# Output projections of blocks 0 and 1, in quarters between the last value products of attention

## The chip, the core and the metric

The kernel runs on one core of a Trainium2 chip. Its engines are named as the profile names them: PE (TensorE; PEld is its weight load), DVE (VectorE), ACT (ScalarE), POOL (GpSimd) and SP (SyncE, which here issues DMAs). The metric is the device time of one execution in microseconds; lower is better.

## The reference

A transformer block on x of shape (4, 2048, 256), all in float32. What matters here is its middle:

```python
h = layernorm(x) * (1 + ca) + sa
# attention: 16 heads of width 16, causal softmax, q and k with rope
y = einsum('bhqk,bhkd->bhqd', softmax(q k^T / 4), v)
x = x + ga * (y.reshape(b, t, 256) @ Wc)          # the output projection
h = layernorm(x) * (1 + cb) + sb
# router: 12 experts (8 with a feed-forward of 512, 4 "zero" ones), top 2
x = x + gb * ffn(h)
```

## The kernel before, in words

Four phases follow one another, each one block of instruction streams per engine, closed by a barrier of all engines (line 978 is the barrier that closes attention's): `project` (norm, q, k, v), `attention`, `route` (output projection, residual, norm, router, sort by expert) and `experts`.

**Attention** works through 16 iterations (4 batch entries x 4 groups of 4 heads). One iteration has 40 tiles of 128 keys by 512 queries: 4, 8, 12 and 16 tiles for the four query ranges of 512, the last four of each range on the diagonal, 512, 384, 256 and 128 queries wide. For a tile PE writes scores (line 1199, four products in strips of 32 rows for each head, one PSUM bank for 512 columns; three banks in turn, 0 to 2), ACT takes the exponential into SBUF (line 1247; one for each bank), POOL masks a diagonal tile (line 1127), and PE adds the tile's value product into bank 3 (line 1215: four heads, 8 records, as each float32 product shows twice). Scores wait for the exponential three banks back. After a query range ACT copies bank 3 (line 1239) and SP stores it (line 1026). Row maxima for the softmax are found beforehand by products into banks 4 to 7 (line 230) and reductions on DVE (line 243); those of the last iteration end long before its last tiles. The order of scores, value products and maxima on PE is a list, `course.pe_order`, which a planner (`Course`) writes from estimated costs; SP's pieces (loads and stores) are hung on value products by `PIECES`. In the last iteration these are the loads for routing: for each of blocks 0 to 3 of 512 tokens, two loads of attention's outputs (line 1474) and one of the rows of x (line 1493), behind value products 1, 4, 7, 10 and so on up to 35. The list ends:

```
scores(36,3) scores(37,0..3) scores(38, heads 0-1) values(36)
scores(38, heads 2-3) scores(39, all heads) values(37) values(38) values(39)
```

Up to value product 35 the four sets of one tile stand between two value products, as in the rows below: values(32), scores(33,3), scores(34,0), (34,1), (34,2), values(33).

Behind the list PE projects block 0 (`projected`, line 1486): for each of its four quarters of 128 tokens two products of 128 x 128 by 128 x 256 in float32 (4 records), into banks 4 and 5. It first waits for the weights (`wc_done`), the loads of block 0 and the last reduction. SP ends its stream with waits for its stores, those of the reciprocals of the softmax sums (line 1013) among them.

**Routing** takes 16 blocks of 512 tokens. PE's order in step s is: projection of block s (line 1611; even blocks into banks 4 and 5, odd ones into 6 and 7), router logits of block s-3 (line 1628), transposes of the normed block s-2 (line 1619). `output(0)` is empty, as attention has done that work. A projection waits for its loads and, from block 2 on, for DVE's residual of the block two before. DVE adds the residual (line 1687, waits for `out_done`), takes statistics, and shifts the normed block (line 1680) after ACT (line 1779) and POOL (line 1820). SP loads block 4 once `out_done` counts 1 and block 5 once it counts 2, each behind its stores of earlier blocks.

Of the kernel before, what the change touches and what calls it, by code (L numbers as in the profile page):

```python
# [31 lines left out]
B, T, C = 4, 2048, 256  # L32
H, L, DH = 16, 64, 16
KC = C // P
# [5 lines left out]
TPB = BLK // P  # L40
# [4 lines left out]
NIT = B * NG  # L45
# [28 lines left out]
ZTERMS = [GROUPS_OF[2][:2], GROUPS_OF[2][2:], GROUPS_OF[0] + GROUPS_OF[1]]  # L74
part_of = [p for p, n in enumerate(PARTS) for _ in range(n)]
XB, XR = 4, 6
BIG = 1e30


def apart(eng):  # L80

    eng.nop(nofuse=True)
# [794 lines left out]
def attention(nc, a, d, k, ps, g0, first, retired):  # L877
    with ExitStack() as ctx:
# [15 lines left out]
        NKT = len(KT)  # L894
# [49 lines left out]
        num, x_in = routed_inputs(k)  # L944
# [13 lines left out]
        red_ready, red_done = g0["red_ready"], g0["red_done"]  # L958
# [19 lines left out]
        with nc.Block() as block:  # L978
# [185 lines left out]
            @block.tensor  # L1164
            def _(pe):
                def group(n, u, at):

                    r = n % R
                    if u == 0:
                        pe.wait_ge(ld[r], LD * (n // R + 1))  # L1170
                    if at >= NRED:
                        pe.wait_ge(red_done, at - NRED + 1)
                    unit_products(pe, k, ps, ks[r], qs[r], u, at).then_inc(red_ready, 1)

                def turn(n, q, at):

                    pe.wait_ge(part_step, PART * (NJ * n + q + 1))
                    pe.wait_ge(red_done, at - NRED + 1)
                    apart(pe)
                    o = red_ps[0:MROWS * QUARTER, at % NRED, 0, :].bitcast(BF16)  # L1180
                    rows = mparts[:, q, :, :, :].rearrange("p h m i -> p (h m i)")
                    for lo in range(0, MROWS * QUARTER, SLOT):
                        part = slice(lo, min(lo + SLOT, MROWS * QUARTER))
                        ins = pe.transpose(o[part, 0:P], rows[:, part], k["identb"][:, :])
                    ins.then_inc(red_ready, 1)

                def scores(n, r, s):

                    m, h0, nh = SETS[s]
                    J, j, lo = KT[m]  # L1190
                    o = st_view(r, s)
                    if s == 0 and 0 < n < R:
                        pe.wait_ge(ones_ld, 16 * (R - 1))
                    if h0 == 0 and j == 0:
                        pe.wait_ge(m_ld, M_LD * (NJ * n + J + 1) + 1)
                    pe.wait_ge(exp_done, NSET * n + s + 1)
                    for h in range(nh):
                        for at_q in QUADS:
                            ins = pe.matmul(o[at_q, h, :], ks[r][0:SROWS + MROWS, h0 + h, j * P + at_q.start:j * P + at_q.stop],  # L1199
                                            qs[r][0:SROWS + MROWS, h0 + h, J * QJ + lo:(J + 1) * QJ], start=True, stop=True)  # L1200
                    ins.then_inc(st_ready, 1)

                def values(n, r, m):

                    J, j, lo = KT[m]
                    if m == 0:
                        pe.wait_ge(v_ld[r], 16 * NV * (n // R + 1))
                    if j == 0:
                        pe.wait_ge(o_done, NJ * n + J + 2)
                    if m in DIAG:  # L1210
                        pe.wait_ge(mask_done, len(DIAG) * n + DIAG.index(m) + 1)
                    else:
                        pe.wait_ge(exp_done, NSET * n + of_tile[m][-1] + 1 + NST)
                    for g in range(HG):
                        ins = pe.matmul(o_ps[SLOT * g:SLOT * (g + 1), lo:QJ], vs[:, r, j, SLOT * g:SLOT * (g + 1)],  # L1215
                                        probs[:, (NKT * r + m) % NPB, g, 0:QJ - lo], start=(j == 0), stop=(m == LAST[J]))
                    ins.then_inc(pv_done, 1)

                for kind, n, x in course.pe_order:
                    if kind == "scores":  # L1220
                        scores(n, n % R, x)
                    elif kind == "values":
                        values(n, n % R, x)
                    elif kind == "turn":
                        turn(n, x, unit_at[n, TURN + x])
                    elif n > 0 or x >= HEAD:
                        group(n, x, unit_at[n, x])
                pe.wait_ge(wc_done, B)
                pe.wait_ge(first["o"][0], 16 * KC)
                pe.wait_ge(red_done, len(course.stream))  # L1230
                apart(pe)
                projected(pe, k, projected_bank(ps, 0), num, 0).then_inc(first["out"][0], 1)

            @block.scalar
            def _(act):
# [241 lines left out]
def projected_bank(ps, j):  # L1477

    return ps[:, 4 + 2 * j:6 + 2 * j, :].rearrange("p n (j c) -> p (n j) c", j=2)


def projected(pe, k, o, num, t):

    for n in range(TPB):
        for c in range(KC):
            ins = pe.matmul(o[:, n, :], num[:, t % XB, c, n * P:(n + 1) * P], k["wc"][:, t // BPS, c, :],
                            start=(c == 0), stop=(c == KC - 1))
    return ins
# [7 lines left out]
def route(nc, a, d, k, r, w, w_in, w_ld, ps, out, scat, first, retired):  # L1496
    with ExitStack() as ctx:
# [41 lines left out]
        with nc.Block() as block:  # L1539
# [61 lines left out]
            @block.tensor  # L1601
            def _(pe):
                def output(t):
                    if t == 0:
                        return
                    pe.wait_ge(o_ld[t % XB], 16 * KC * (t // XB + 1))
                    if t >= RAW:
                        pe.wait_ge(y_done, t - RAW + 1)
                    if t >= 2:
                        pe.wait_ge(mid_done, t - 1)  # L1610
                    projected(pe, k, pc[t % 2], num, t).then_inc(out_done, 1)

                def normed(t):
                    pe.wait_ge(mod_done, t + 1)
                    if t >= 1:
                        pe.wait_ge(ht_done, t)
                    for n in range(TPB):
                        for c in range(KC):
                            ins = pe.transpose(pd[:, n, c, :], r["h2"][:, TPB * t + n, c * P:(c + 1) * P], k["ident"][:, :])
                    ins.then_inc(tr_done, 1)  # L1620

                def logits(t):
                    pe.wait_ge(ht_done, t + 1)
                    if t >= 1:
                        pe.wait_ge(lgb_done, t)
                    for n in range(TPB):
                        for c in range(KC):
                            ins = pe.matmul(pl[:, n, :], h2_t[:, n, c, :], k["gate"][:, c, :], start=(c == 0), stop=(c == KC - 1))
                    ins.then_inc(lg_done, 1)

                def counts(*parts):
                    def stage(t):
                        for p in parts:
                            if t == LASTS[p]:
                                pe.wait_ge(c_ld, 16 * len(CONSTS))
                                pe.wait_ge(oh_done, p + 1)
                                if p > 0:
                                    pe.wait_ge(pos_done, 2 * p)
                                chains[p].counts(pe, r, bank).then_inc(cnt_mm, 1)
                    return stage  # L1640

                def weights(lo, hi):
                    def stage(t):
                        e = t - (NB - E)
                        if not lo <= e < hi:
                            return
                        for half in range(4):
                            m, h, n = half // 2, half % 2, 4 * e + half
                            if h == 0:
                                pe.wait_ge(w_ld[m][e % 2], 16 * (e // 2 + 1))  # L1650
                            if n == 0:
                                pe.wait_ge(mid_done, NB)
                            if n >= 4:
                                pe.wait_ge(wt_copy, n - 3)
                            for q in range(4):

                                at = (q * KC + h) * P if m == 0 else ((q % 2) * FC + 2 * h + q // 2) * P
                                ins = pe.transpose(ps[:, 4 + half, q * P:(q + 1) * P], w_in[:, e % 2, m, at:at + P], k["ident"][:, :])
                            ins.then_inc(wt_done, 1)
                    return stage  # L1660

                blocks((6, counts(0, 2)), (AT + 1, counts(1)), (0, output), (3, logits), (8, weights(0, 1)), (2, normed), (8, weights(1, E)))
# [521 lines left out]
```

## Time and profile before

| | us |
|---|---|
| median of 3 runs | 2433.78 |
| lowest, highest | 2430.32, 2438.25 |
| the profiled execution, whole | 2438.3 |
| its span | 2436.6 |
| PE busy, share of the span | 2294.7, 94% |
| DVE, ACT, POOL busy | 1875.3, 1675.1, 727.1 |
| mean granted clock of PE | 0.975 of 2.4 GHz |

All rows below come from the one profiled execution, counted in microseconds from the start of its span. A product's record runs over the start of the next one, since products are pipelined: the time that PE gives to a group is read from its start to the start of what follows. In a timeline, the bracket at the end gives the idle time of the engine ahead of the row and what ended it; "PEq L978" is the closing of attention's barrier. In windows the columns are width, then for each engine busy time and (x) number of records, then granted clock, share of the DMA engines and GB/s; if one engine is named, its busy time stands alone. Attention ends at some 1794 us, routing follows.

### The profile page before, as it was taken

How to read it: one execution, taken by the hardware profiler on the slowest of the kernel's cores; microseconds unless marked ns; L12 is line 12 of the kernel's file. 1: busy time of each engine (PE TensorE's matmuls, PEld its weight loads, DVE VectorE, ACT ScalarE, POOL GpSimd, SP SyncE). 2: the span in 40 equal slices, each digit the busy share in tenths (PEclk: the TensorE clock that was granted, in tenths of full speed). 3: DMA queues.
4: the chain of work that ended last, by engine and by line, in shares of the span. 5: the costliest groups of instructions: out<-in, count | busy, mean ns of one | idle time of the engine just before them, and what ended most of it. 6: DMA issues, size and time to landing. Idle time of an engine off the chain costs nothing. (4 is left out here: it accounts for less than half of the span.)

```text
span 2436.6 us, 84929 instructions
## 1 busy us (share of the span) xinstructions
PE 2294.7 (94%) x34552; PEld 1502.4 (62%) x34553; DVE 1875.3 (77%) x3209; ACT 1675.1 (69%) x3057; POOL 727.1 (30%) x878
## 2 busy tenths in 40 slices
PE   7887789999999999999999999999989799999998
PEld 4554345555555555555555555555458698889897
DVE  5887779889898898898898898898548743655664
ACT  4776347778778788778888887878864454545554
POOL 2333211111111111111111211211225567686454
PEclk9999789999999999999999999999998899999999
DMA  7898553253442543543543532320357665665565
GB/s 206 236 269 228 113 96 98 74 121 87 107 100 84 115 95 87 109 98 82 114 100 80 114 91 64 86 64 21 90 170 234 222 126 109 114 133 101 94 107 87
DMA packets 224670, 287.95 MB, mean 118 GB/s; under 512 B 29478, under 2 KB 177990, under 8 KB 223942
## 3 DMA queue, kind: packets, MB, share of 16 engines
q1 hardware_dynamic: 185324, 235.53, 38.3%
q0 software_dynamic: 31872, 41.30, 9.9%
q10 hardware_dynamic: 7136, 6.32, 0.9%
q8 instruction: 247, 4.05, 0.8%
q14 instruction: 91, 0.75, 0.1%
HBM read 143.37 MB, written 138.81 MB: 116 GB/s over the span
## 5 line engine op out<-in xcount | busy, mean ns | idle before, releaser
L243 DVE TENSOR_REDUCE mxc<-ps 128x2 f32<-128x1024 f32 (+4 forms) x1168 | 1283.0, 1147 | 179.9 <-PE ps L230 98.2
L1247 ACT ACTIVATE probs<-ps 128x512 f32<-128x512 f32 (+1 forms) x2240 | 1164.6, 589 | 323.9 <-PE ps L1199 307.6
L1215 PE MATMUL ps<-probs,vs 128*32 128x512 f32 (+3 forms) x5120 | 600.1, 529 | 3.4 <-issue 2.6
L230 PE MATMUL ps<-ks,qs 96*32 96x512 bf16 (+12 forms) x7040 | 495.6, 346 | 35.3 <-DMA qs<-q_parts 16.1
L1199 PE MATMUL ps<-qs,ks 99*32 99x512 bf16 (+3 forms) x7040 | 510.7, 350 | 10.2 <-ACT probs L1247 4.8
L230 PEld LDWEIGHTS ps<-ks,qs 96*32 96x32 bf16 x7040 | 209.4, 97 | 273.0 <-DVE mxc L243 108.0
L1127 POOL TENSOR_SCALAR_AFFINE_SELECT probs<-probs 128x512 f32<-128x512 f32 x256 | 161.1, 637 | 601.1 <-ACT probs L1247 599.7
L1199 PEld LDWEIGHTS ps<-qs,ks 99*32 99x32 bf16 x7040 | 212.5, 96 | 168.6 <-ACT probs L1247 85.9
L1976 PE MATMUL ps<-x_t,w_at 128*128 128x128 f32 x1968 | 242.8, 277 | 4.4 <-ACT w_at L2021 4.4
L2107 POOL DMA_INDIRECT out<-ys,idx x120 | 192.3, 1603 | 146.3 <-DMA out<-ys,idx 88.6
L1976 PEld LDWEIGHTS ps<-x_t,w_at 128*128 128x128 f32 x1968 | 231.6, 193 | 6.1 <-ACT w_at L2021 6.0
L1199 PE MATMUL ps<-shared 99*32 99x512 bf16 (+3 forms) x3200 | 230.6, 348 | 0.6 <-ACT probs L1247 0.3
L1985 PE MATMUL ps<-w2t,hid_t 128*128 x960 | 227.9, 380 | 2.6 <-ACT hid_t L2013 1.6
L1215 PEld LDWEIGHTS ps<-probs,vs 128*32 128x32 f32 x5120 | 183.2, 110 | 70.9 <-issue 4.0
L230 PE MATMUL ps<-shared 96*32 96x512 bf16 (+11 forms) x3200 | 220.7, 341 | 4.6 <-DVE mxc L243 3.4
L1111 POOL CAST mparts<-negm 128x16 bf16<-128x16 f32 x64 | 12.7, 198 | 647.8 <-DVE negm L1266 647.8
L2076 DVE TENSOR_TENSOR ys<-ps,gm 128x256 f32<-128x256 f32 x120 | 50.9, 425 | 186.4 <-PE ps L1985 133.3
L1985 PEld LDWEIGHTS ps<-w2t,hid_t 128*128 128x128 f32 x960 | 173.2, 190 | 22.7 <-issue 4.0
L2021 ACT COPY w_at<-shared 128x1024 f32 x126 | 131.8, 1046 | 52.6 <-issue 49.2
L230 PEld LDWEIGHTS ps<-shared 96*32 96x32 bf16 x3200 | 96.5, 96 | 109.6 <-DVE mxc L243 44.8
L1437 POOL DMA_INDIRECT slot_x<-h,pos x128 | 131.4, 1027 | 61.3 <-issue 38.3
L235 PEld LDWEIGHTS ps<-mask_qk,identb 128*32 128x32 bf16 x4096 | 138.1, 98 | 10.7 <-issue 1.5
(178 smaller groups left out, 2173.6 us busy)
## 6 DMA issues: line engine op xcount, KB each, us to landing
ks<-k_parts SPq DMA_DIRECT2D x66, 256.0 KB, 4.2
qs<-q_parts SPq DMA_DIRECT2D x66, 256.0 KB, 4.2
xs<-slot_x SPq DMA_DIRECT2D x126, 131.0 KB
v_ones<-vout SPq DMA_DIRECT2D x64, 256.0 KB, 4.4
vs<-v_ones SPq DMA_DIRECT2D x64, 256.0 KB, 3.2
attn_t<-o_sb SPq DMA_DIRECT2D x64, 256.0 KB, 3.3
slot_x<-zero SPq DMA_DIRECT2D x48, 262.0 KB, 2.6
q_parts<-parts SPq DMA_DIRECT2D x96, 128.0 KB
```

The lines of the kernel that those rows point to most:

```text
L230: ins = pe.matmul(o[at_q, h, 0:n], qs[0:SROWS, h0 + h, i * P + at_q.start:i * P + at_q.stop], ks[0:SROWS, h0 + h, 512 * c:512 * c + n], st ...
L235: ins = pe.matmul(o[at_q, h, w - P + at_q.start:w], k["identb"][:, at_q], k["mask_qk"][:, at_q.start:P], start=False, stop=True, skip_grou ...
L243: return dve.tensor_reduce(mxc[:, h0:h0 + nh, i, c], unit_view(ps, u, at), AX_X, ALU.max)
L1127: pool.affine_select(at, at, pattern=[[0, HG], [1, P]], base=0, channel_multiplier=-1, compare_op=ALU.is_ge, fill=keep).then_inc(mask_done, 1)
L1199: ins = pe.matmul(o[at_q, h, :], ks[r][0:SROWS + MROWS, h0 + h, j * P + at_q.start:j * P + at_q.stop], qs[r][0:SROWS + MROWS, h0 + h, J * ...
L1215: ins = pe.matmul(o_ps[SLOT * g:SLOT * (g + 1), lo:QJ], vs[:, r, j, SLOT * g:SLOT * (g + 1)], probs[:, (NKT * r + m) % NPB, g, 0:QJ - lo], ...
L1247: act.activation(probs[:, (NKT * r + m) % NPB, h0:h0 + nh, 0:QJ - lo], st_view(r, s), ACT.Exp, scale=DH ** -0.5).then_inc(exp_done, 1)
L1437: pool.indirect_dma_start(d[f"slot_x{p}"][:, :], bass.IndirectOffsetOnAxis(ap=r["pos"][c][:, t:t + 1], axis=0), r["h2"][:, t, :], None).th ...
L1976: ins = pe.matmul(ph[:, q, f * P:(f + 1) * P], w1_at[:, q, c, f * P:(f + 1) * P], x_t[:, q, c, :], start=(c == 0), stop=(c == KC - 1))
L1985: ins = pe.matmul(py[:, q, 0:C], h_t[:, q, f, :], w["w2t"][:, bass.ds(e, 1), f, :].rearrange("p o c -> p (o c)"), start=(f == 0), stop=(f ...
L2021: act.copy(w1_at[:, q, :, :], w["w1t"][:, bass.ds(e, 1), :, :].rearrange("p o c f -> p (o c) f")).then_inc(w1_done[p], 1)
L2107: pool.indirect_dma_start(rows, bass.IndirectOffsetOnAxis(ap=idx[:, p, t:t + 1], axis=0), ys[:, t % YR, :], None, compute_op=ALU.add).then ...
```

## The change

The projection of block 0 is no longer issued behind the list, and that of block 1 no longer in routing. The eight quarters of the two blocks are issued one each behind value products 32 to 39 of the last iteration. The waits that stood ahead of block 0's projection stand ahead of the first quarter, those for the loads of a block ahead of its first. The last quarter of each block counts `out_done` up. In routing `output(t)` is empty for blocks 0 and 1. Nothing else is moved; the planner doesn't know of the quarters.

```diff
--- before.py
+++ after.py
@@ -74,6 +74,7 @@
 ZTERMS = [GROUPS_OF[2][:2], GROUPS_OF[2][2:], GROUPS_OF[0] + GROUPS_OF[1]]
 part_of = [p for p, n in enumerate(PARTS) for _ in range(n)]
 XB, XR = 4, 6
+EARLY_OUT = 2
 BIG = 1e30
 
 
@@ -1216,20 +1217,30 @@
                                         probs[:, (NKT * r + m) % NPB, g, 0:QJ - lo], start=(j == 0), stop=(m == LAST[J]))
                     ins.then_inc(pv_done, 1)
 
+                def projected_early(i):
+
+                    t, n = divmod(i, TPB)
+                    if n == 0:
+                        pe.wait_ge(first["o"][t], 16 * KC)
+                    if i == 0:
+                        pe.wait_ge(wc_done, B)
+                        pe.wait_ge(red_done, len(course.stream))
+                        apart(pe)
+                    ins = projected(pe, k, projected_bank(ps, t), num, t, [n])
+                    if n == TPB - 1:
+                        ins.then_inc(first["out"][0], 1)
+
                 for kind, n, x in course.pe_order:
                     if kind == "scores":
                         scores(n, n % R, x)
                     elif kind == "values":
                         values(n, n % R, x)
+                        if n == NIT - 1 and x >= NKT - EARLY_OUT * TPB:
+                            projected_early(x - (NKT - EARLY_OUT * TPB))
                     elif kind == "turn":
                         turn(n, x, unit_at[n, TURN + x])
                     elif n > 0 or x >= HEAD:
                         group(n, x, unit_at[n, x])
-                pe.wait_ge(wc_done, B)
-                pe.wait_ge(first["o"][0], 16 * KC)
-                pe.wait_ge(red_done, len(course.stream))
-                apart(pe)
-                projected(pe, k, projected_bank(ps, 0), num, 0).then_inc(first["out"][0], 1)
 
             @block.scalar
             def _(act):
@@ -1479,9 +1490,9 @@
     return ps[:, 4 + 2 * j:6 + 2 * j, :].rearrange("p n (j c) -> p (n j) c", j=2)
 
 
-def projected(pe, k, o, num, t):
-
-    for n in range(TPB):
+def projected(pe, k, o, num, t, tiles=range(TPB)):
+
+    for n in tiles:
         for c in range(KC):
             ins = pe.matmul(o[:, n, :], num[:, t % XB, c, n * P:(n + 1) * P], k["wc"][:, t // BPS, c, :],
                             start=(c == 0), stop=(c == KC - 1))
@@ -1601,7 +1612,7 @@
             @block.tensor
             def _(pe):
                 def output(t):
-                    if t == 0:
+                    if t < EARLY_OUT:
                         return
                     pe.wait_ge(o_ld[t % XB], 16 * KC * (t // XB + 1))
                     if t >= RAW:
```

## Rows read from the trace of the kernel before

**Rows 1.** The page: its span, and the chain that ended last

```profile
span 2436.6 us, 84929 instructions
...
PE 17%; another core or an unknown queue 1%; issue 1%; DMA 0%; ACT 0%; ACTq 0%; SPq 0%; DVE 0%; POOL 0%; DVEq 0%; POOLq 0%
```

**Rows 2.** Windows of two stages: width, busy time per engine, clock, DMA

```profile
1770.00:1784.00 14.00, 12.11 (x160) 3.70 (x160) 0.00 (x0) 13.31 (x26) 0.00 (x0) 1.00 0.16 40
1813.00:1837.00 24.00, 24.00 (x160) 22.25 (x159) 21.96 (x101) 13.43 (x24) 8.59 (x5) 1.00 0.96 281
```

**Rows 3.** Timeline, one tile of scores: start, length, engine, line, [idle before <-releaser]

```profile
1773.06 1.03 PE L1215 MATMUL ps<-probs,vs 128*32 128x512 f32 x8
...
1773.92 0.82 PE L1199 MATMUL ps<-qs,ks 99*32 99x512 bf16 x12
...
1775.01 0.40 PE L1199 MATMUL ps<-qs,ks 99*32 99x512 bf16 x4 [0.27 <-ACT probs L1247]
...
1775.24 1.03 PE L1215 MATMUL ps<-probs,vs 128*32 128x512 f32 x8
```

**Rows 4.** ACT in windows of 0.05 us within that tile

```profile
1774.20:1774.25 0.05, 0.05 (x1) 1.00 0.77 287
1774.25:1774.30 0.05, 0.00 (x0) 1.00 0.86 328
```

**Rows 5.** Timeline, the last value products and the end of attention

```profile
1787.77 0.62 PE L1199 MATMUL ps<-qs,ks 99*32 99x256 bf16 x24
...
1788.21 0.85 PE L1215 MATMUL ps<-probs,vs 128*32 128x384 f32 x8
1788.21 1.08 ACT L1247 ACTIVATE probs<-ps 128x512 f32<-128x512 f32 x2 [0.33 <-PE ps L1199]
...
1789.62 1.02 PE L1215 MATMUL ps<-probs,vs 128*32 128x256 f32 x16 [0.56 <-POOL probs L1127]
1790.21 0.16 PEld L1215 LDWEIGHTS ps<-probs,vs 128*32 128x32 f32 x8 [0.43 <-POOL probs L1127]
...
1790.57 3.72 PE L1486 MATMUL ps<-wc,shared 128*128 128x256 f32 x16
...
1791.71 0.43 SPq L1013 DMA_DIRECT2D rden<-rec  x1
```

**Rows 6.** Waits of SP from 1785 to 1800 us: total, times, longest

```profile
SPq L1100 <- DMA rden<-rec: 1.7, 1, 1.7
SPq L978 <- PEq L978: 0.4, 1, 0.4
```

**Rows 7.** Timeline, routing's first blocks

```profile
1794.62 7.14 PE L1486 MATMUL ps<-wc,shared 128*128 128x256 f32 x32 [0.33 <-PEq L978]
1794.73 0.38 DVE L1761 MEMSET h<- 128x384 f32 x1 [51.49 <-PEq L978]
...
1795.14 1.23 DVE L1687 TENSOR_TENSOR shared<-ps,shared 128x1024 f32<-128x1024 f32 x1
...
1804.88 1.97 PE L1619 MATMUL ps<-ident,h 128*128 128x128 f32 x8 [3.11 <-DVE h L1680]
...
1806.64 4.17 PE L1486 MATMUL ps<-wc,shared 128*128 128x256 f32 x16
...
1810.85 1.23 DVE L1687 TENSOR_TENSOR shared<-ps,shared 128x1024 f32<-128x1024 f32 x1 [1.17 <-PE ps L1486]
...
1813.26 3.62 PE L1486 MATMUL ps<-wc,shared 128*128 128x256 f32 x16
...
1816.72 1.85 PE L1628 MATMUL ps<-gate,h_t 128*128 128x12 f32 x16
```

**Rows 8.** PE in windows of 0.5 us: width, busy, granted clock, DMA

```profile
1804.00:1804.50 0.50, 0.00 (x0) 0.84 0.89 289
1804.50:1805.00 0.50, 0.12 (x1) 0.50 1.01 352
...
1807.50:1808.00 0.50, 0.50 (x3) 0.74 1.11 268
```

## The prediction

> **What bounds the kernel now.** I went from the page to the stage. The chain of waits that ended last reaches back over less than a fifth of the span [rows 1], into the experts, and says nothing of the place of the change; so it has to be read from the stretch around the end of attention. The windows there show two different stages [rows 2]: the last value products (PE 12.11 of 14.00 us busy, ACT 13.31, DVE and POOL idle) and, in routing, a stretch in which PE is busy for all 24.00 us of 24.
>
> The timeline of one tile of the score loop [rows 3] shows the order: behind a value product come three scores sets (12 products), a wait, the fourth set (4 products) and the next value product. The period is 2.18 us (value products at 1773.06 and 1775.24). It is a loop through two engines, not the throughput of either: the value product holds PE from 1773.06 to 1773.92 (0.86 us), the first scores set behind it starts at 1773.92, its exponential must end before the fourth set may have its bank, and that set starts at 1775.01 (1.09 us later, with 0.27 us of idle PE "<-ACT probs"); the next value product follows at 1775.24 (0.23). 0.86 + 1.09 + 0.23 = 2.18. Is there room on ACT's side? The narrow windows [rows 4] show ACT busy up to 1774.25 and then idle: it waits for that first set. The three scores banks are empty when the value product ends. So nothing lies in store that would cover more PE work at this place.
>
> At the very end [rows 5] the masks of POOL release the last value products: 1788.21, 1789.62 and 1790.21 us, with PE idle between. Then PE projects block 0 (1790.57, 3.72 us, to 1794.29), beside ACT's copy and SP's two stores (the second at 1791.71). SP waits 1.7 us for the store of the reciprocals and then 0.4 us for PE at the line that closes the block (L978) [rows 6]. So the projection at the end of attention is nearly free already: PE is later than SP by 0.4 us.
>
> In routing [rows 7] PE projects blocks 1 and 2 in one row of 7.14 us from 1794.62, and then waits 3.11 us for DVE's first normalised block. DVE's first residual starts at 1795.14, and nothing waits for block 1's projection.
>
> **The change, part by part.**
>
> (a) *Removed: block 0's projection behind attention.* Sixteen records, 3.72 us, of which only the 0.4 us by which SP waits for PE lie on the path. Gain: 0.4 us. It can't be more, since SP's own chain (value product, copy, store, landing) keeps its length.
>
> (b) *Removed: block 1's projection from routing,* some 3.5 us of PE (half of the 7.14). It lies before a 3.11 us wait of PE for DVE [rows 7], so PE only waits longer. DVE's chain starts with block 0's result in both kernels. SP's waits for the two results aren't last either: its store of block 0 needs DVE. Gain: 0.
>
> (c) *Added: eight quarters of 2 products (4 records) each.* A full block takes 3.46 us from its start to the start of the next work (1813.26 to 1816.72) [rows 7], 0.865 us a quarter; the block at the end of attention gives 3.72 / 4 = 0.93 [rows 5]. I take 0.865, as the row of work that runs on, and keep 0.93.
>
> Quarters 0 to 3 stand behind value products 32 to 35, before the scores set for which ACT already waits [rows 3, 4]. Each stretches the loop by its whole length: 4 x 0.865 = 3.46 us. That PE idles 0.27 us a tile doesn't help, because this idle time comes behind the exponential that is itself made late.
>
> Quarter 4 stands between value product 36 and the last scores (1787.77). Before, ACT idles 0.33 us for these scores already [rows 5], and its exponentials lead to the last masks: +0.865.
>
> Quarter 5 falls between value products 37 and 38, which start 1.41 us apart (1788.21, 1789.62). Product 37 is 384 wide, 0.86 x 384 / 512 = 0.64 us; 0.64 + 0.865 - 1.41 = +0.10.
>
> Quarter 6 falls between 38 (256 wide, 0.43 us) and 39, which start 0.59 us apart: 0.43 + 0.865 + 0.10 - 0.59 = 0.80 in all, so +0.70 over the 0.10.
>
> Quarter 7 comes behind the last value product, beside the copy, two DMA issues and their landing, which take over 3 us (PE's 3.72 us was only 0.4 late); 0.865 is hidden. Without that cover it would cost 0.865.
>
> The last value product is late by 3.46 + 0.865 + 0.10 + 0.70 = 5.13 us, and with it the copy, the stores and the end of the block.
>
> (d) *Waits.* The waits for weights, the loads and all reductions move ahead of quarter 0. The reductions' banks are free: DVE has been idle for 51.49 us at 1794.73 [rows 7], so since 1743.2, and quarter 0 comes at about 1778. The loads of both blocks are issued behind value products 4, 13 and earlier ones, 19 tiles of some 2.18 us ahead. In front of quarter 0 stands one empty instruction as before. I take 0; between 0 and 0.33 us, the idle time of PE behind the block's close (at 1794.62) [rows 7], as the largest thing of this kind. SP's loads of block 3's rows and ACT's and POOL's work wait for the value products, so they are late by the same 3 to 5 us; block 3's rows are wanted at 1810.85, some 20 us later.
>
> (e) *The clock in routing.* Before, PE's wait of 3.11 us is followed by a granted clock that falls to 0.50, the lower level of 1.2 GHz, from about 1804.3 us to 1807.8 [rows 8]; the block projected across its end takes 4.17 us against 3.62 later [rows 7]. After the change PE has nothing from the end of quarter 7 to DVE's first residual: about 4.7 us around the close of the block (in the times of before, quarter 7 ends at 1790.43 + 0.865 = 1791.3 and is 5.13 later; the residual ends at 1796.4 and is 4.7 later). The clock may thus fall there too. But only block 2's projection runs in it, at worst 2 x 3.46 = 6.9 us, and it has 1804.88 - 1796.4 = 8.5 us until PE's next work. What counts is the clock at that next work, low before as well. I take 0. The ends are a gain of 1.2 us (DVE's wait for PE at 1810.85 is gone) and a loss of 1.7 us (another 3.5 us at half the clock).
>
> **Sum:** 5.13 - 0.4 = +4.7 us. The profiled execution would go from 2438.3 us (span 2436.6) to 2443.0. That execution is 4.5 us above the median of the three runs, so I put the same step on the median: 2433.8 + 4.7 = **2438.5 us**, +0.19%. With 0.93 us a quarter it would be +5.2, and the rivals give the outer ends. About 0.3% (7.3 us) is what a measurement of this kernel can tell from no change, so the forecast is "same", on the slow side.
>
> **Rivals.**
>
> 1. *A switch between narrow and whole-array products costs something (slower).* Value products and scores write strips of 32 rows, the projection uses the whole array. Place: both sides of every quarter, where PE would have to empty before it loads. With a quarter of q us (q over 0.77) the steps above add up to 7q - 0.93. Slower by 7.3 us begins at 7q - 0.93 - 0.4 = 7.3, so q = 1.23. If on entry one weight load (3.32 / 16 = 0.21 us) and the 0.16 us by which a product's record outlives its turn (3.62 - 3.46) are paid, and 0.1 on leaving, q = 1.33: +8.0 us, 2441.8. For it: the block at 1790.57 starts 0.15 us behind the streaming of product 39 (1790.21, 128 wide: 0.86 x 128 / 512 = 0.21) [rows 5]. Against it: there stood waits and an empty instruction as well. Chance 0.15.
>
> 2. *No weight load of a quarter is hidden.* Then q = 0.865 + 4 x 0.21 = 1.70 and the steps give 7 x 1.70 - 0.93 - 0.4 = +10.6 us, 2444.4. Against it: in a block from 1813.26 to 1816.72, 16 products of 0.216 us spacing leave no room for 16 loads in a row beside them unless both run at once. Chance 0.03. The Trainium skill has a rule that asks for this: TensorE: Matmul & The Clock Gate, Part 3, "The mechanism", says that a weight load overlaps running products only when its row group differs from theirs, and whole-array products share all rows. By that rule the time would be this rival's 2444.4 us; the trace disagrees with it inside a block.
>
> 3. *The quarters partly hide in PE's idle time.* If the loop were bound by ACT's throughput, PE's idle 0.40 us a tile (2.18 less 0.86 and four sets of 0.23) would take a part of each of the first four: 0.465 instead of 0.865, 1.6 us less. +3.1 us, 2436.9. For it: ACT's 13.31 of 14.00 us. Against it: ACT's gap [rows 4]. Chance 0.12.
>
> 4. *Routing wins from a PE that is ahead.* PE is full in routing's later part [rows 2], and the 3.46 us of block 1 come off: +4.7 - 3.5 = +1.2 us, 2435.0. Against it: PE's wait of 3.11 us wipes out any lead. Chance 0.07.
>
> 5. *The clock stays low longer at the start of routing.* +1.7 us on top: +6.4, 2440.2. For it: PE's idle time before its first work in routing grows from nothing to 4.7 us. Against it: at that time PE isn't last. Chance 0.12.
>
> That a part doesn't do what it says (waits that hold it at the end) would give about no change; 0.03.
>
> **How the numbers follow.** Forecast 0.48, rivals 1 to 5 0.15, 0.03, 0.12, 0.07 and 0.12, the rest 0.03. The range reaches down past rivals 3 and 4 and up past rivals 1 and 5, and takes in that single runs before lie between 2430.3 and 2438.3 us: 2433 to 2444. Slower by over 0.3%: rival 1 nearly whole (0.12), rival 2 (0.03), half of rival 5 (0.06), and 0.05 for a forecast that is 2.6 us too low: 0.26. Faster by over 0.3% would need 12 us less than forecast, which no part can give: 0.03. Same: 0.71.
>
> **What would show it.** In the changed kernel: value products 32 to 35 some 3.05 us apart instead of 2.18, with ACT idle about 0.9 us more in each tile and put down to scores; PE idle between value products 38 and 39 gone; the last copy of ACT 5.1 us later by the loop's own clock; SP no longer waiting for PE at the end of the block but PE for SP; routing's first residual to first transposes unchanged at 9.7 us. The forecast is wrong if the tiles stay below 2.7 us (rival 3), reach 3.4 us (rivals 1, 2), or if the stretch from the first residual to 1837 us before changes by more than 1 us (rivals 4, 5).

## The result and the profile after

| us | before | after |
|---|---|---|
| median (20 runs each) | 2434.52 | 2439.06 |
| lowest, highest | 2429.35, 2439.87 | 2434.7, 2443.37 |
| the profiled execution, its span | 2438.3, 2436.6 | 2440.21, 2438.5 |
| mean granted clock | 0.975 | 0.975 |

The ratio is 1.0016, with a 95% interval from 1.0009 to 1.0024: 2.2 to 5.8 us slower, 3.9 by the ratio and 4.5 by the medians. The difference is small, but the interval doesn't hold 1. Forecast were 4.7 us.

The whole is too coarse to test the steps, so all of them are read from the stretch between two marks that both kernels have, called the stage below: the start of value product 32 of the last iteration, and ACT's first instruction of routing (the load of its table). The marks before:

```profile
1777.42 1.03 PE L1215 MATMUL ps<-probs,vs 128*32 128x512 f32 x8
...
1794.58 1.28 ACT L1772 ACT_TABLE_LOAD   x1 [3.29 <-PEq L978]
```

That is **17.16 us**. After, it is 1785.27 to 1809.56 (both rows stand below), **24.29 us**: 7.13 us more, not 4.7. One tile of it, PE and ACT, answers to [rows 3, 4]:

```profile
1785.27 1.03 PE L1216 MATMUL ps<-probs,vs 128*32 128x512 f32 x8
...
1786.23 0.73 PEld L1497 LDWEIGHTS ps<-wc,shared 128*128 128x128 f32 x4 [0.84 <-issue]
1786.23 1.13 PE L1497 MATMUL ps<-wc,shared 128*128 128x256 f32 x4
...
1787.29 0.83 PE L1200 MATMUL ps<-qs,ks 99*32 99x512 bf16 x12
1787.74 1.57 ACT L1258 ACTIVATE probs<-ps 128x512 f32<-128x512 f32 x3 [1.29 <-PE ps L1200]
...
1788.39 0.40 PE L1200 MATMUL ps<-qs,ks 99*32 99x512 bf16 x4 [0.27 <-ACT probs L1258]
...
1788.62 0.60 PE L1216 MATMUL ps<-probs,vs 128*32 128x512 f32 x4
```

The value products now start 3.35 us apart (1785.27, 1788.62), where 2.18 had been. Follow PE: 0.96 us from the value product to the quarter, 1.06 for the quarter (L1497), 1.10 from the first scores set to the fourth, 0.23 to the next value product. The third and fourth of these are as before (1.09, 0.23). ACT's row shows who pays: it idles 1.29 us for the scores, where it idled about 0.1 us. The quarter costs 1.06 and not 0.865 us, and the value product in front of it ends 0.10 us later than by the loop's own 0.86. Together a place costs 1.17 us.

The last value products and the end of attention, against [rows 5]:

```profile
1799.45 1.03 PE L1216 MATMUL ps<-probs,vs 128*32 128x512 f32 x8
...
1801.92 0.82 PE L1216 MATMUL ps<-probs,vs 128*32 128x384 f32 x8
1801.93 1.09 ACT L1258 ACTIVATE probs<-ps 128x512 f32<-128x512 f32 x2 [1.50 <-PE ps L1200]
...
1803.73 0.64 PE L1216 MATMUL ps<-probs,vs 128*32 128x256 f32 x8
...
1805.37 0.42 PE L1216 MATMUL ps<-probs,vs 128*32 128x128 f32 x8
...
1805.72 1.13 PE L1497 MATMUL ps<-wc,shared 128*128 128x256 f32 x4
...
1806.86 0.43 SPq L1014 DMA_DIRECT2D rden<-rec  x1
1809.56 1.28 ACT L1783 ACT_TABLE_LOAD   x1 [3.12 <-PEq L979]
```

Product 39 starts at 1805.37, 20.10 us behind product 32; before it was 1790.21 - 1777.42 = 12.79. So it comes 7.31 us late, where 5.13 were forecast. "[... <-POOL probs]" is gone from PE's rows: the quarters fill the waits for the masks and more. From product 39 to ACT's first instruction of routing it is 4.19 us instead of 4.37. SP's waits there, against [rows 6]:

```profile
SPq L1101 <- DMA rden<-rec: 1.7, 1, 1.7
SPq L979 <- PEq L979: 0.2, 1, 0.2
```

SP still shows a wait for PE, of 0.2 instead of 0.4 us, but it is no longer for PE's work: the last record of PE's products ends at 1806.85, over 2 us ahead of the end of the block. In e_halves below, where PE has nothing to do behind value product 39, the same row shows 0.2 us as well. So of the 0.4 us before only some 0.2 were block 0's projection, and they are gone; the rest belongs to the closing of the block. Routing's first rows of PE and of DVE, against [rows 7]:

```profile
1811.49 5.84 PE L1497 MATMUL ps<-wc,shared 128*128 128x256 f32 x16 [4.64 <-DVE shared L1698]
1819.86 1.09 PE L1630 MATMUL ps<-ident,h 128*128 128x128 f32 x8 [2.53 <-DVE h L1691]
```
```profile
1810.12 1.23 DVE L1698 TENSOR_TENSOR shared<-ps,shared 128x1024 f32<-128x1024 f32 x1
```

From DVE's first residual (1810.12) to the first transposes (1819.86) it is 9.74 us, as before (1795.14 to 1804.88): that block 1's projection is gone from here gains nothing. PE's projection of block 2 waits 4.64 us for DVE and then takes 5.84 us, most of it at the low clock, and no residual of DVE waits for it. The transposes take 1.09 us, against 1.97 in the profile before, and from the first residual to the one later row in which PE waits 0.85 us for DVE it is 45.48 us instead of 46.86. Its row before, and below it after:

```profile
1842.00 1.93 PE L1628 MATMUL ps<-gate,h_t 128*128 128x12 f32 x16 [0.85 <-DVE lg L1708]
```
```profile
1855.60 1.93 PE L1639 MATMUL ps<-gate,h_t 128*128 128x12 f32 x16 [0.85 <-DVE lg L1719]
```

That is 1.4 us which routing seems to give back. The experiments below show that both values come up in both kernels.

### The profile page after: what moved, and what is told of

It is laid out like the page before. It is cut to its first block and busy times, and to the rows that moved or that the text cites. A ratio compares the mean times of both kernels' runs of the same rounds, so it can differ in the third digit from the quotient of the medians.

```text
span 2438.5 us, 84929 instructions
## 1 busy us (share of the span) xinstructions
PE 2292.2 (94%) x34552; PEld 1493.6 (61%) x34553; DVE 1877.2 (77%) x3209; ACT 1676.9 (69%) x3057; POOL 726.1 (30%) x878
## 5 line engine op out<-in xcount | busy, mean ns | idle before, releaser
L2028 ACT COPY x_t<-ps 128x256 f32<-128x256 f32 x126 | 46.8, 372 | 160.5 <-PE ps L1979 158.4
```

## The experiments

Two marks in routing are used as well: "stretch R" is that from the first residual to the router logits with the 0.85 us wait. The experiments ran on three chips, one for each set that was run together, and each whole time is compared with runs of the kernel before on the same chip. Each kernel's edit is against the kernel before or after, as said.

### Both kernels once more

> The kernel before once more, for the spread between two executions of the same program. The stage of the change (start of value product 32 of the last iteration to ACT's first instruction of routing) took 17.16 us in the first profile and should repeat within 0.2 us. From the first residual of routing to the first logits for which PE waits 0.85 us for DVE it took 46.86 us; if the clock level at the first transposes is a matter of where PE's idle times fall, 46.9 again. Open: how far the start of value product 32 (1777.4 us) and the time of the experts move from one execution to the next; if the changed kernel's later start of product 32 (7.9 us) and its faster experts (11 us) are chance, this run should move by several us as well.

> The changed kernel once more. The stage of the change took 24.29 us in its first profile, 7.1 more than before, and the stretch in routing 45.48, 1.4 less. Both should repeat within 0.2 us if they are the change's own; start of value product 32 and the experts should move by several us if those are chance.

| profile | product 32 at | stage | first transposes | stretch R | first residual to end |
|---|---|---|---|---|---|
| before, first | 1777.42 | 17.16 | 1.97 | 46.86 | 641.5 |
| before, second | 1781.54 | 17.17 | 1.97 | 47.11 | 634.9 |
| after, first | 1785.27 | 24.29 | 1.09 | 45.48 | 628.4 |
| after, second | 1780.22 | 24.29 | 1.97 | 47.13 | 632.6 |

The stage repeats within 0.01 us. What lies ahead of it and the experts behind it move by 4 to 7 us between executions of one kernel, so the 7.9 us by which product 32 came later in the first pair can be chance (in the four profiles of each kernel it starts at 1777.4 to 1782.6 us before and at 1780.2 to 1786.6 after, ranges that overlap), and no difference of two spans says anything on a change of this size. The stretch in routing went to 47.13 us in the second profile of the changed kernel, so the 1.4 us are chance too, or not always there. The granted clock is what changed with it. PE in windows of 1 us of the changed kernel's second profile (width, busy time and records, granted clock, DMA):

```profile
1812.00:1813.00 1.00, 0.57 (x3) 1.00 0.61 117
1813.00:1814.00 1.00, 0.00 (x0) 1.00 0.80 233
1814.00:1815.00 1.00, 0.19 (x1) 0.90 1.06 374
1815.00:1816.00 1.00, 1.00 (x6) 0.50 1.09 392
```

PE is idle in the second row, the transposes start at 1814.81, and the clock is at its lower level, 1.2 GHz, from there on (0.50).

### Where a quarter's price comes from: e_halves

```diff
-                        if n == NIT - 1 and x >= NKT - EARLY_OUT * TPB:
-                            projected_early(x - (NKT - EARLY_OUT * TPB))
+                        if n == NIT - 1 and NKT - 8 <= x < NKT - 4:
+                            for i in range(2):
+                                projected_early(2 * (x - (NKT - 8)) + i)
```

> The eight quarters stand in pairs behind value products 32 to 35, none behind 36 to 39. Theory 1 (the products of a quarter cost 0.865 us, and each place where PE goes from strips to the whole array and back costs about 0.3 us once): value products 32 to 35 4.2 us apart (2.18 + 2 x 0.865 + 0.31), stage 17.2 + 4 x 2.04 - 0.4 = 24.9 us, the whole 7.8 us less what routing gives back over the kernel before. Rival (the products themselves are slower here, 1.17 us a quarter wherever it stands): 4.5 us apart, stage 26.2 us. If the quarters were partly hidden in idle time of PE: under 3.9 us apart.

PE's timeline:

```profile
1783.38 1.03 PE L1216 MATMUL ps<-probs,vs 128*32 128x512 f32 x8
1784.34 1.99 PE L1498 MATMUL ps<-wc,shared 128*128 128x256 f32 x8
1786.26 0.83 PE L1200 MATMUL ps<-qs,ks 99*32 99x512 bf16 x12
1787.37 0.40 PE L1200 MATMUL ps<-qs,ks 99*32 99x512 bf16 x4 [0.27 <-ACT probs L1259]
1787.59 1.03 PE L1216 MATMUL ps<-probs,vs 128*32 128x512 f32 x8
```

The value products are 4.21 us apart (1783.38, 1787.59, and 1791.81 next), where theory 1 asked for 4.2 and the rival for 4.5. Two quarters in a row take 1.92 us (1784.34 to 1786.26), one takes 1.06: the second costs 0.86, the price taken from routing, and the first 0.20 more. With the 0.10 us in front of it that is the price of a place, 0.3 us. A place here is a spot where PE goes from products in strips to whole-array ones and back; the two passages are called seams. The stage is 25.14 us (24.9 expected; the 0.4 us at the close of the block were counted as won, and 0.16 were). The whole is 1.0033 of before (1.0018 to 1.0048), 4.4 to 11.7 us more, which holds the stage's 8.0.

### Is it the loop? e_third

```diff
                         scores(n, n % R, x)
+                        if n == NIT - 1 and SETS[x][1:] == (1, 1) and NKT - 6 <= SETS[x][0] < NKT - 2:
+                            projected_early(SETS[x][0] - (NKT - 6))
...
-                        if n == NIT - 1 and x >= NKT - EARLY_OUT * TPB:
+                        if n == NIT - 1 and x >= NKT - TPB:
```

> Quarters 0 to 3 stand behind the third of the four scores sets of a tile, ahead of the set for which PE waits for ACT, instead of behind the value product; quarters 4 to 7 as in the changed kernel. Theory 1 (the loop value product, first set, its exponential, fourth set is what sets the tile): the quarter takes the place of PE's wait, 2.9 us a tile instead of 3.35 (fourth set 1.8 us behind the first instead of 1.1), stage 24.3 - 4 x 0.45 = 22.5 us. Rival (a quarter costs its 1.17 us wherever it stands): 3.35 us a tile, stage 24.3 us.

```profile
1783.23 1.03 PE L1216 MATMUL ps<-probs,vs 128*32 128x512 f32 x8
...
1784.09 0.82 PE L1200 MATMUL ps<-qs,ks 99*32 99x512 bf16 x12
...
1784.84 1.13 PE L1499 MATMUL ps<-wc,shared 128*128 128x256 f32 x4
...
1785.90 0.40 PE L1200 MATMUL ps<-qs,ks 99*32 99x512 bf16 x4
...
1786.13 1.03 PE L1216 MATMUL ps<-probs,vs 128*32 128x512 f32 x8
...
1787.43 1.57 ACT L1260 ACTIVATE probs<-ps 128x512 f32<-128x512 f32 x3 [0.48 <-PE ps L1200]
```

The same quarter, moved by three scores sets, gives tiles of 2.90 us (1783.23, 1786.13) instead of 3.35; ACT idles 0.48 us for the scores instead of 1.29. The first and the fourth set are 1.81 us apart, as computed. So it is the place within the loop that decides: behind the value product a quarter pays in full, ahead of the fourth set it takes over PE's wait for ACT. PE's own work is then the bound (the row has no idle time), and a quarter still costs 0.72 us. The stage is 21.94 us (22.5 expected). The difference is the fourth place: products 35 and 36 are 3.12 us apart, against 4.12 in the changed kernel and 2.94 before, so that quarter costs 0.18 us and not 0.72. The whole: 1.0014 (1.0001 to 1.0026), 0.2 to 6.3 us over before, with 4.8 from the stage. Its transposes take 1.46 us and stretch R 47.19.

### Parts of the change: e_end, e_one

e_end, against the changed kernel, puts all eight quarters behind the list (and none between value products); e_one only sets the number of early blocks to one.

```diff
-                        if n == NIT - 1 and x >= NKT - EARLY_OUT * TPB:
-                            projected_early(x - (NKT - EARLY_OUT * TPB))
...
+                for i in range(EARLY_OUT * TPB):
+                    projected_early(i)
```

```diff
-EARLY_OUT = 2
+EARLY_OUT = 1
```

> Both blocks behind the last value product, none between value products. Theory (SP's stores cover 0.4 us less than one block): the stage 17.2 + 3.5 = 20.6 us, PE last at the close of the block by 3.9 us; no seam costs between value products. Routing: block 1's projection gone again wins nothing by itself; PE's idle time ahead of the first transposes is 4.9 us instead of 3.1, so the clock is low there as before: 46.9 us for the stretch in routing, or more. Whole: +3.5 us, 2438. Rival (the routing part wins from a PE that is ahead): the stretch 3.5 us shorter, whole +0.

> Only block 0 in quarters, behind value products 36 to 39; block 1 in routing as before. Theory: 36 costs 1.17 us, 37 0.40, 38 0.9 to 1.05, 39 nothing, less 0.2 at the close of the block: stage 17.2 + 2.4 = 19.6 us. Routing as before, clock low at the first transposes: 46.9 us. Rival (the gain of routing comes from an earlier barrier's idle time and not from block 1's projection): 45.5.

SP's waits at the end of attention in e_end:

```profile
SPq L979 <- PEq L979: 3.0, 1, 3.0
SPq L1101 <- DMA rden<-rec: 1.3, 1, 1.3
```

e_end: value products 2.18 us apart as before, one row of 7.17 us of projections behind the last, and SP waits 3.0 us for PE (3.9 had been expected; SP itself is slower, its issue of the last store takes 1.59 us instead of 0.43). Stage 20.62 us, expected 20.6. Block 1's projection is 3.46 us wherever nothing hides it, and routing's wait of PE for DVE is a place where it is hidden: first residual to first transposes 9.73 us again. Stretch R is 45.48 us, where 46.9 or more had been expected: no low clock at the transposes here. Whole 1.0023 (1.0008 to 1.0039), 1.9 to 9.5 us; the rival's +0 is out.

In e_one PE's rows show the last four places by themselves:

```profile
1788.92 1.03 PE L1216 MATMUL ps<-probs,vs 128*32 128x512 f32 x8
1789.88 1.13 PE L1497 MATMUL ps<-wc,shared 128*128 128x256 f32 x4
1790.94 0.63 PE L1200 MATMUL ps<-qs,ks 99*32 99x256 bf16 x24
1791.40 0.82 PE L1216 MATMUL ps<-probs,vs 128*32 128x384 f32 x8
1792.15 1.13 PE L1497 MATMUL ps<-wc,shared 128*128 128x256 f32 x4
1793.21 0.64 PE L1216 MATMUL ps<-probs,vs 128*32 128x256 f32 x8
1793.78 1.13 PE L1497 MATMUL ps<-wc,shared 128*128 128x256 f32 x4
1794.84 0.42 PE L1216 MATMUL ps<-probs,vs 128*32 128x128 f32 x8
1795.19 1.13 PE L1497 MATMUL ps<-wc,shared 128*128 128x256 f32 x4
```

Products 36 to 37 are 2.48 us apart (1.31 before), 37 to 38 1.81 (1.41), 38 to 39 1.63 (0.59): +1.17, +0.40, +1.04. Stage 19.61 us, as expected (19.6). The whole is 1.0006 (0.9993 to 1.0018), no difference that can be told. Its stretch R was 45.48 us and not 46.9: the expected low clock did not come. The rival asked for this value, but the profiles below show that one profile can't decide it.

### The clock at routing's first transposes: e_hold, and more profiles

e_hold, against the kernel before, moves no work; it only lets PE's projection of block 1 wait for the first residual.

```diff
                     if t >= 2:
                         pe.wait_ge(mid_done, t - 1)
+                    if t == 1:
+                        pe.wait_ge(mid_done, 1)
```

> The kernel before, with one wait more: in routing PE starts block 1's projection only when DVE has ended the first residual. No work is moved. PE's idle time ahead of the first transposes is then 1.8 us ahead of the projections and 1.3 us behind them, instead of 3.1 in one piece. Theory (what routing gave back in the changed kernel is the granted clock at the first transposes): no low clock there, transposes 1.07 us instead of 1.97, stretch 45.5 instead of 46.9 us, first residual to first transposes 9.7 as before; the whole 1.4 us less, too little to be told. Rival (the gain came from block 1's projection being gone): 46.9 us. Stage of attention's end 17.2 us.

```profile
1801.63 7.14 PE L1486 MATMUL ps<-wc,shared 128*128 128x256 f32 x32 [2.22 <-DVE shared L1689]
1810.37 1.09 PE L1621 MATMUL ps<-ident,h 128*128 128x128 f32 x8 [1.59 <-DVE h L1682]
```

The idle time is split (2.22 and 1.59 us, planned were 1.8 and 1.3), the transposes take 1.09 us, stretch R is 45.86 us. The first residual to the first transposes is 10.11 us, 0.4 more than expected, since DVE's second residual now waits for block 1's projection. Stage 17.16. The whole is 0.9998 of before (0.9986 to 1.0011). One profile at the full clock doesn't prove the theory, since the kernel before might reach it too. So both kernels were profiled again, and the changed one timed again:

> Third profile of the kernel before. Stage 17.16 us. Open between: the first transposes of routing always meet the low clock in this kernel (stretch 46.9 to 47.1 us, transposes 1.97 us), or by chance (then 45.5 us, 1.07 us in some profiles). From the first residual to the end of the span, 641.5 and 634.9 us so far: if these are chance around the same mean as in the changed kernel (628.4 and 632.6), this one may lie anywhere from 628 to 642.

> Fourth profile of the kernel before, with the same two questions as the third.

> Fourth profile of the changed kernel: stage 24.29 us; the stretch in routing 45.5 or 47.1 us, of which each was seen once; from the first residual to the end of the span 628 to 634 us.

> The changed kernel timed again, to set its whole time against its stage: the stage at the end of attention is 7.1 us longer in both profiles so far, the whole 4.5 us by the medians of the first 20 runs, with an interval that ends at 5.8. Theory A (routing and the experts give some 2 to 3 us back): again +2 to +6 us. Theory B (nothing is given back, the first comparison lay low by chance): +7 us. Routing's stretch: 45.5 or 47.1 us, whichever clock level the first transposes meet.

| profile | stage | first transposes | stretch R | first residual to end |
|---|---|---|---|---|
| before, third | 17.17 | 1.97 | 46.95 | 650.0 |
| before, fourth | 17.16 | 1.09 | 45.52 | 649.0 |
| after, third (timed) | 24.29 | 1.10 | 45.49 | 648.9 |
| after, fourth | 24.29 | 1.09 | 45.50 | 647.9 |

The fourth profile of the kernel before shows the full clock at the transposes, with the same idle time ahead of them; PE's timeline there, and below it that of the second profile:

```profile
1809.37 1.09 PE L1619 MATMUL ps<-ident,h 128*128 128x128 f32 x8 [3.13 <-DVE h L1680]
```
```profile
1809.01 1.97 PE L1619 MATMUL ps<-ident,h 128*128 128x128 f32 x8 [3.12 <-DVE h L1680]
```

Same program, 3.13 and 3.12 us of idle PE, and transposes of 1.09 and 1.97 us. In the kernel before it is chance whether the clock falls at this wait: it did in 3 of 4 profiles. In the changed one, where the wait is 2.2 to 3.0 us long, it did in 1 of 4, and of the five other kernels only in e_third (transposes of 1.46 us, the lower clock from their middle on). Whether the change moves the odds can't be said from four profiles each; e_hold's theory is neither shown nor refuted.

On the chip of this last set the whole took some 19 us more before (median 2453.14) and 21 more after (2460.58) than in the first comparison, with the same stage; most of it lies behind the first residual, in both kernels. The ratio is 1.0027 (1.0014 to 1.0040), 3.4 to 9.8 us; 6.6 by the ratio, 7.4 by the medians. It holds the stage's 7.1 us and lies nearer to theory B (nothing is given back, +7) than to A (+2 to +6), without ruling A out. The first comparison, with its upper end at 5.8, does not; the two intervals overlap from 3.4 to 5.8 us.

## Why the prediction was right, and where it wasn't

**The forecast held**: slower by less than the 0.3% that the prediction took as its limit, 2439.06 us against 2438.5. The mechanism is shown: a quarter behind a value product stretches a loop through PE and ACT, and is not taken up by PE's idle time (e_third; rival 3 is out, with tiles of 3.35 us where it asked for under 2.7). The tiles were forecast at 3.05 us, and 3.4 would have been the sign of rivals 1 and 2: they lie nearer to the sign than to the forecast.

**Part (c) was sized too low.** The step that failed is "I take 0.865": the price of a quarter within a row of whole-array products. That term was mis-sized: a single quarter between products in strips costs 1.17 us. This was rival 1's mechanism, at two thirds of its size (0.30 us a place instead of 0.46). The arithmetic of the steps was sound: its formula 7q - 0.93 gives 7.26 us with q = 1.17, and 7.31 were measured. The trace of before had it. PE's timeline narrowed to the first product of the block at the end of attention, before:

```profile
1790.57 0.48 PE L1486 MATMUL ps<-wc,shared 128*128 128x256 f32 x1
```

and narrowed to the first and the last product of the first quarter, after:

```profile
1786.23 0.48 PE L1497 MATMUL ps<-wc,shared 128*128 128x256 f32 x1
```
```profile
1786.98 0.38 PE L1497 MATMUL ps<-wc,shared 128*128 128x256 f32 x1
```

A first product's record is 0.48 us long, the others' 0.38. The last one starts at 1786.98 and the scores follow at 1787.29, 0.31 us later, where products in a row are 0.216 apart. In the prediction the 0.10 us within the first product stayed unread, and the 0.15 us ahead of it I took for waits. Where PE comes to a block from whole-array transposes there is no such price. Before, narrowed to the first product of the block at 1813.26:

```profile
1813.15 0.30 PEld L1486 LDWEIGHTS ps<-wc,shared 128*128 128x128 f32 x2
1813.26 0.38 PE L1486 MATMUL ps<-wc,shared 128*128 128x256 f32 x1
```

The load starts 0.11 us ahead of the product and the record has the usual 0.38 us; at a seam load and product start together (both at 1786.23). So the price goes with strips beside whole-array products, and an exposed weight load would fit it; no run separates that from other costs of the passage. Rival 2 (every load paid in full, 1.70 us a quarter) is out: the second quarter of a pair costs 0.86 us, so weight loads within a row of whole-array products are hidden. That disagrees with the rule that the prediction weighed (the Trainium skill, TensorE: Matmul & The Clock Gate, Part 3, "The mechanism": a weight load overlaps running products only when its row group differs), but not with the section's other sentence, by which a load into the background weight buffer may go ahead of running products too; no run here shows which buffer a load went to. What a seam costs beyond such a row is 0.10 us ahead, 0.10 us within the first product and 0.09 us on the way back.

**Part (a)**: 0.18 us gained where 0.4 were forecast, since about 0.2 of SP's 0.4 us belong to the closing itself and not to PE's work (e_halves). The sign "SP no longer waiting for PE" is met in that sense only. **Part (b)**: nothing gained, as forecast; rival 4 is out (9.74 us in both kernels, and e_end). **Part (d)**: nothing seen; the first quarter costs no more than the next (products 32 to 33: 3.35 us, as 33 to 34). **Part (e)**: PE's idle time around the close of the block does bring the low clock (0.50 from 1810 to 1815 in the first profile after), and block 2's projection takes 5.84 us across its end, hidden as forecast. At the transposes, which part (e) put at nothing because the clock was low before as well, it is low in some profiles of both kernels. The prediction's sign of being wrong, a stretch in routing that changes by over 1 us, thus did appear in the first pair (1.4 us) without rival 4 or 5 behind it; rival 5's extra 1.7 us are in none of the four profiles after (45.5 or 47.1 us, as before).

**So the whole came out near the forecast partly by luck.** The stage is 7.1 us longer, in all four profiles of the changed kernel against all four of the one before. The forecast had 4.7 us for it, 2.4 too few. That the first comparison gave 4.5 us can come from the clock in routing (0.7 us, if its odds are what four profiles each show) and from the scatter of the whole; what else is in it stays open. The second comparison gives 6.6 us by its ratio, where the first gave 3.9.

No kernel of this study beats the kernel before beyond what can be told; e_hold's 0.9998 is equal to it, and every one that moved projections was longer at its stage.

## What to carry to other kernels

Idle time of an engine is room for more work only if nothing that waits for the inserted work sets the pace. In a loop that runs through two engines, work placed right ahead of the instruction that the other engine is waiting for pays in full; the same work ahead of an instruction that itself waits pays less (here 0.72 instead of 1.17 us). Before moving work off the end of a phase, look at what covers it there: here all but 0.2 us of it was free. And take the price of a small piece from where pieces of its kind meet others, not from the middle of a long row: the seams were a quarter of the cost.

## What the runs showed of the hardware

- Going from 32-row strips to a whole-array float32 product and back costs PE about 0.3 us in all: 0.10 us before the first product, 0.10 us within it (its record 0.48 us long where 0.38 is usual), 0.09 us before the next strip product. It is paid for each place, not for each product (e_halves: 1.06 us for one quarter, 1.92 for two), and not between whole-array transposes and the projection (0.38 us records).
- An idle wait of PE of 3.1 us ahead of the same instruction brings PE's clock down to 1.2 GHz in some executions of one program and not in others (3 of 4 and 1 of 4 profiles of the kernel before). The cost here is 1.3 to 1.6 us (45.5 against 46.9 to 47.1), 0.06% of the kernel.
- Between single executions of one program the start of value product 32 moved by 5 to 6 us and the time behind the first residual by up to 6.6 us (the record doesn't say whether the first profiles are of the second ones' chip; between the two profiles of each kernel known to be of one chip these are 0.7 and 4.0 us, and 1.0 us in both), while a stretch of 17 or 24 us at the end of attention repeated within 0.01 us. A change of some microseconds is to be read from its own stretch.
